# Attention with gated feed-forward on Trainium2: 41 maxima pieces a group in another order of pieces, and 68 instead of 55 ahead of the first score piece

## The reference

```python
xn = _layernorm(x, axis=-1)
s = _L0_attn_ref(xn, w_qkv, b_qkv, w_out, b_out)      # softmax(q k / 4 + alibi + causal) v, then w_out
g = _silu(_L0_ffn_ref(xn, w_gate, w_up, w_down))      # down(silu(gate(x)) * up(x)), ternary weights
x = x + s * g
```

## Time and profile before

| | us |
|---|---|
| median of 3 runs | 844.55 (843.7 to 845.68) |
| the profiled execution, its own time | 842.03 |
| its span in the trace | 840.0 |
| PE busy | 799.9 (95%) |
| DVE busy | 637.3 (76%) |
| ACT busy | 468.9 (56%) |

### The profile page before, as it was taken

The page is one execution under the profiler, slowest core; times in us unless marked ns, Lnnn a source line. Parts: engine busy times, 40 slices in busy tenths (PEclk is TensorE's granted clock), DMA queues, the critical chain, the costliest instruction groups (busy, mean ns, idle before and its releaser), DMA issues.

```text
span 840.0 us, 16103 instructions
## 1 busy us (share of the span) xinstructions
PE 799.9 (95%) x5926; PEld 352.8 (42%) x5926; DVE 637.3 (76%) x1822; ACT 468.9 (56%) x615; POOL 120.9 (14%) x136
## 2 busy tenths in 40 slices
PE   5999999999999999999899999999999999999998
PEld 3444545444444444444344343443434334343333
DVE  6656877733533565664899999999999999997546
ACT  5425275333132232222488888888888788787540
POOL 4213132223032131121000000000000005500000
PEclk9999999999999999999799999999999999999999
DMA  7474322358202101101121122222125333654636
GB/s 251 139 197 182 128 101 76 107 128 297 103 1 82 69 1 47 54 0 52 51 70 54 56 72 80 79 67 74 55 63 161 91 92 104 195 132 129 215 132 222
DMA packets 71055, 88.40 MB, mean 105 GB/s; under 512 B 26926, under 2 KB 37166, under 8 KB 70464
## 3 DMA queue, kind: packets, MB, share of 16 engines
q1 hardware_dynamic: 70848, 87.10, 32.4%
q0 software_dynamic: 128, 0.27, 0.2%
HBM read 51.15 MB, written 35.93 MB: 104 GB/s over the span
## 4 chain that ended last, share of the span: by engine, by line
PE 62%; DVE 23%; issue 7%; DMA 4%; ACT 3%; SPq 0%; POOL 0%; DVEq 0%; ACTq 0%
PE psum L1515 9%; PE psum L1492 9%; PE psum L1516 9%; DVE mx L1158 9%; DVE mshown L1154 8%; PE psum L1449 7%; PE psum L1526 5%; PE psum L1527 5%; PE psum L1467 2%; DVE mx L1154 2%; PE psum L1346 2%; PE psum L1348 2%; PE psum L1347 2%; PE psum L1550 1%; PE psum L1360 1%
## 5 line engine op out<-in xcount | busy, mean ns | idle before, releaser
L881 ACT ACTIVATE probs<-psum,exp_scale 128x1024 f32<-128x1024 f32 (+1 forms) x320 | 310.6, 1028 | 80.0 <-PE psum L1476 60.0
L1154 DVE CUSTOM_DVE_ANT_0 mshown<-psum,ahead 128x384 bf16<-128x384 f32 (+3 forms) x512 | 219.2, 487 | 1.4 <-PE psum L1449 0.4
L1449 PE MATMUL psum<-QKs 51*128 51x512 f16 (+3 forms) x768 | 189.0, 334 | 18.4 <-DVE mx L1158 6.2
L1492 PE MATMUL psum<-probs,Vs 128*32 128x512 f32 (+3 forms) x1536 | 162.1, 510 | 0.2 <-ACT probs L881 0.2
L1158 DVE TENSOR_REDUCE mx<-psum 128x1 f32<-128x512 f32 x256 | 157.6, 681 | 2.7 <-PE psum L1449 1.7
L1467 PE MATMUL psum<-QKs 53*128 53x512 f16 (+3 forms) x768 | 140.0, 331 | 1.6 <-ACT probs L881 1.4
L1515 PE MATMUL psum<-X,room 128*128 128x512 f16 (+1 forms) x352 | 133.6, 379 | 0.0
L1516 PE MATMUL psum<-X,room 128*128 128x512 f16 (+1 forms) x352 | 133.4, 379 | 0.0
L1449 PEld LDWEIGHTS psum<-QKs 51*128 51x128 f16 x768 | 51.9, 94 | 157.1 <-DVE mx L1154 85.6
L906 ACT ACTIVATE room<-psum,gate_half 128x512 f32<-128x512 f32 (+1 forms) x44 | 30.3, 688 | 101.2 <-PE psum L1516 101.2
L757 POOL TENSOR_TENSOR room<-room 128x512 f16<-128x512 f32 (+1 forms) x44 | 50.9, 1157 | 174.5 <-ACT room L911 174.5
(11 more groups left out here) (161 smaller groups left out, 912.7 us busy)
## 6 DMA issues: line engine op xcount, KB each, us to landing
o_scr<-osum SPq DMA_DIRECT2D x32, 256.0 KB, 3.1
QKs<-q_scr SPq DMA_DIRECT2D x96, 64.0 KB
QKs<-k_scr SPq DMA_DIRECT2D x96, 64.0 KB
q_scr<-qk_stage SPq DMA_DIRECT2D x16, 256.0 KB, 2.3
k_scr<-qk_stage SPq DMA_DIRECT2D x16, 256.0 KB, 2.2
v_scr<-v_stage SPq DMA_DIRECT2D x16, 256.0 KB, 2.1
Vs<-v_scr SPq DMA_DIRECT2D x16, 256.0 KB
probs<-in_L_attn_x SPq DMA_DIRECT2D x4, 1024.0 KB, 11.2
```

The costliest lines, as they stand in the source:

```text
L881: nc.scalar.activation(probs[n % PSLOTS][:, 2 * pair:2 * pair + 2, 0:COLS[n]], s_bank[pair][:, :, 0:COLS[n]], ACT.Exp, scale=exp_scale[:, ...
L1154: last = nc.vector.tensor_tensor_reduce(out=mshown[at % 2][:, cols], in0=m_bank[bank][:, cols], in1=ahead[:, CH - keys:], scale=1.0, scala ...
L1449: last = nc.tensor.matmul(tile[:, hh, :], Qs[s][rows, pair + hh, qb * P:(qb + 1) * P], Ks[s][rows, pair + hh, k0:k0 + keys], start=(hh == ...
L1492: last = nc.tensor.matmul(pv_bank[32 * h:32 * h + 32, CH - cols:CH], Vs[s][:, kb, h::QH], probs[n % PSLOTS][:, h, at:at + cols], start=(kb ...
```

## The change

`GROUP` has 41 M instead of 42, in another order with the 20 S and 10 P. The items no longer begin at the same place in each group: `line(t)` gives the first one, 25 items into quad 1 for group 0, 24 into quad 2 for group 1, and so on to 11 into quad 15 for group 14. So the items put between the tiles of the gated stage are 66 instead of 52, and with the M of group 0 that stand ahead of its first score piece 68 instead of 55. The number of items in the whole program, 672, and the instructions of each are unchanged.

```diff
-GROUP = "MPMMPSMMSMPMMSSMMMSSMMPMSMMSPMMSMPMM" \
-        "SMSMMPMSMMMMSSMPMMSPMMSSMMPMMSMSMMSM"
+GROUP = "MPMSMPMMPMSMMSMMSMMSMSMMMSMPMSMSMPM" \
+        "MPMSSMMPMSMMPMSMSMMPMMSSMMPMSMMSMSSM"
+AHEAD = [LEAD + (QUADS - 2 - t) * (NITEM - GROUP.count("M")) for t in range(QUADS - 1)]
+
+
+def line(t):
+
+    return (t + 1) * NITEM + AHEAD[t] if t < QUADS - 1 else QUADS * NITEM
...
-    items = [(t + 1, i) for i in range(LEAD, NITEM)] + [(t + 2, i) for i in range(LEAD)]
+    items = [divmod(i, NITEM) for i in range(line(t), line(t + 1))] if t < QUADS - 1 else []
+    if t == QUADS - 2:
+        items.append((QUADS, ROWS_AT))
...
-    early = [(0, i) for i in range(NITEM) if i != ROWS_AT] + [(1, i) for i in range(LEAD)]
+    early = [divmod(i, NITEM) for i in range(line(0)) if i != ROWS_AT]
```

More of the change, by code:

```diff
@@ L161, in group_order @@
             out.append(("products", *products.pop(0)))
-        else:
+        elif items:
             out.append(("maximum", *items.pop(0)))
-    return [w for w in out if w[1] >= 0 and (w[0] != "maximum" or w[1] < QUADS or w[1:] == (QUADS, ROWS_AT))]
+    return [w for w in out if w[1] >= 0]
 def work_order():
-    early = [(0, i) for i in range(NITEM) if i != ROWS_AT] + [(1, i) for i in range(LEAD)]
+    early = [divmod(i, NITEM) for i in range(line(0)) if i != ROWS_AT]
     tiles = [(j, p) for j in range(NCH) for p in range(FTILES)]
```

## The result

| | before | changed | ratio |
|---|---|---|---|
| median of the runs | 844.12 us (843.14 to 845.68) | 893.44 us (888.96 to 897.49) | 1.0579, 95% interval 1.055 to 1.0609 |
| span of the profiled execution | 840.0 | 890.9 | |
| mean granted clock of TensorE | 0.99 | 0.959 | |

The kernel is 49 us slower. Forecast were 20 us, 864.5 with a range up to 876. The direction was right, and both costs that were summed are there; the size was not, since what the sum left out, the clock above all, is larger than what it had.

A forecast was written before the change was run, and what follows sets the result against it. PE was taken to bound the gated stage and DVE the attention stage, with PE close behind. Terms 14.4 - 7.8 + 13.5 = +20.1 us on the median 844.55 gave 864.5, range 851 to 876.

The forecast's parts named there:

- both costs that were summed: Likeliest case: gated stage (14.4 us) and new order of pieces in attention (13.5) both cost; 856 to 869, chance 0.58.
- the clock: PE's clock might halve behind three new idle stretches in the gated stage, 4.5 to 15 us; left out of the sum.
- rival 3: The clock falls in the gated stage, or PE lags behind its banks in more places: 869 to 880, chance 0.15.
- 13 fewer items: Attention stage: 13 full tiles fewer behind the first score piece, 0.60 us each on the pace-setting engine: -7.8 us.
- (a): Gated stage: 11 more items ahead of the last tile, 0.18 us a fill and 0.1 a break: 2.2 us.
- (d): Behind the gated stage's last tile: six items instead of four, fifth and sixth waiting 0.61 us each: 1.2 us.
- (b): Gated stage: the fourth fill of portions behind three output tiles waits 3.23 us each, less 0.4: 9.3 us.
- (c): Gated stage: the fourth fill behind up tiles (2, 7) and (3, 7) waits 0.92 us each, less 0.13: 1.7 us.
- The covers: Attention: three banked items' reads must cover product piece and next fill; narrow items fall short, +13.5 us, bounds 4 to 18.
- The signs that the prediction named: Profile after: 3.2 us idle PE behind three output tiles, unequal attention groups; half clock between 320 and 400 for rival 3.
- The row item comes earlier than before in all groups but the last ones, with no cost: Attention stage: the row item's earlier place in the groups was priced at 0.
- What is hidden: Attention: ACT's work, the next quad's load and the row item stay covered; 0 taken for the load.

The follow-up runs named there:

- experiment 5: The changed kernel with 15 added matmuls on constants keeping PE busy ahead of each fill that waits about 3 us, at four places: 888.74 us, 1.0518.
- experiment 12: Changed kernel with gated-stage portions of three, fills in the stretch without products done twice, and the last rows' transpose eight pieces later: 862.29 us, 1.0218.
- experiment 1: The changed kernel with at most three items handed out between two tiles of the gated stage, all else as changed: 880.16 us, 1.0424.
- experiment 4: The kernel before with one portion of four behind output tile (2, 22), paid back by a portion of two behind tile (3, 0): 849.65 us, 1.0061.
- experiment 2: The changed kernel with portions of at most three in the gated stage and the old order of pieces less one maximum: 867.22 us, 1.0271.
- experiment 11: experiment 2 with the 41 tiles of maxima in another order, chosen to lower the count of late reads from 16.9 to 11.6 us: 864.61 us, 1.0248.
- experiment 3: The kernel before with the new order of pieces alone, 42 maxima a group, nothing sliding: 886.32 us, 1.0506.
- experiment 6: experiment 3 with the fills of the stretch without products done twice, 11 in each of groups 1 to 13: 862.18 us, 1.021.
- experiment 13: experiment 12 with the loads for GpSimd's first pass over the denominators issued three score-piece steps earlier: 864.31 us, 1.0241.

## Why the prediction was wrong

The step that failed is **the clock**. The prediction had seen that PE's clock fell to half behind the idle stretch at the end of the gated stage, and wrote of the three new ones: "It is a rival below", with nothing in the sum. For the attention stage it did not consider the clock at all. The runs put about 21 us there, as much as the whole forecast of 20; the other 10 us that were missed are spread over the table's five smaller differences.

| part of the 50.9 us | predicted | found |
|---|---|---|
| start, up to tile (2, 0) | 0 | 2.5 |
| gated stage without the clock | 14.4 | 15.6 (21.3 less the 5.7 of experiment 5) |
| half clock in the gated stage | rival 3 | 5.7 |
| half clock in attention | not foreseen | about 15 |
| wait for the last rows, group 14 | 0 | 2.1 |
| GpSimd's pass against DVE, group 12 | 0 | about 1.5 |
| attention, 13 fewer items and late reads | -7.8 + 13.5 = 5.7 | 8, the rest |

How the 15 come about: experiment 12 differs from experiment 1 in attention by -14.0 us (396.6 to 382.6). It has 2.1 us less of waiting for the rows, and its doubled fills cost 3.3 (groups 2, 4, 6 and 7, without half clock in either, are 0.21 to 0.24 longer, times 15). So 14.0 - 2.1 + 3.3 = 15.2 for 41 us less of half clock, 0.37 of each. Group 3 gives the same without a doubled fill: 25.93 with 3.4 us of half clock, 24.65 in experiment 5, where none fell into it, 0.38 of each. In the gated stage it is 5.7 of 13.6, 0.42; 1.1 of the 13.6 lie in a wait, where they cost nothing. In experiment 4, where all of it fell on PE's dense work, it was 1.7 of 3.4, one half. That attention has less than half fits with DVE setting the pace in part of it; this is argued, not measured. The terms are differences of single traces; I hold each to be good to about 1 us, an estimate.

**(a) and (d), more fills and two more items at the end:** right. 3.1 in experiment 1, where their prices give 3.2; the fifth and sixth item 0.60 each.

**(b) Portions of four behind output tiles:** right. Waits of 3.23, 2.97 and 3.23 us, 9.4 against 9.3; and one made alone in the kernel before gave 3.23. What was missing is what each sets off, some 2 us more.

**(c) Behind up tiles:** right. 0.78 and 0.96, 1.7 against 1.7.

**13 fewer items:** not measured by itself. DVE's busy time in a group fell by 0.4 us (24.02 to 23.6), where the step had 0.60, and its idle time in the five groups of the next paragraph rose from 0.23 to between 0.68 and 1.40: the item's time was given back and waits took it up again. No group is shorter than before.

**The covers:** right in kind, too low in size, and weak as a rule. In the five groups after group 0 that had no half clock the step gives 24.24 - 0.60 + 0.6, 0.8, 1.1, 0.5 and 0.7, that is 24.24, 24.44, 24.74, 24.14 and 24.34; measured were 25.00, 24.54, 25.08, 24.28 and 24.46, 0.3 more in the mean, the "further 0.3 in each group" of its upper bound. The waits of DVE for PE's fills in attention, as the traces have them, are 2.1 us before, 25.5 changed (with what the half clock adds), 16.2 in experiment 12 (no half clock after group 0, up to 3.3 from doubled fills) and 23.6 in experiment 2; the count had 1.2, 14.7, 14.7 and 16.9. With LEAD 14 it gave 1.7 for 1.97, with LEAD 22 0.6 for 1.60, and it did not rank two orders of items (experiment 11). It names the mechanism, but its error is as large as the differences between good alignments.

**The signs that the prediction named** were there: idle stretches of 3.2 ahead of fills, groups that differ, the shortest of them 6 and 7, half clock between 320 and 400. Groups 9 and 10 were to be about 25 us and took 26.74 and 28.13, with 3.4 and 6.8 us of half clock. The half clock was named as the mark of rival 3, and that is what came: rival 3 had 869 to 880 and a chance of 0.15, and its price, 5.7 us, is near the 4.5 that the prediction worked out for short falls. Alone it would have left the time within the range; the fall in attention took it out.

**"The row item comes earlier than before in all groups but the last ones, with no cost"** failed in its second half: no cover was named for the last group, where the row now stands directly behind the last item. And GpSimd was missing from "What is hidden" altogether: since the items slide, the closing instructions of a quad come at another time in each group, and one of them met GpSimd's pass.

**Why the clock falls in attention** is shown as far as the order goes: the new order alone does it in each group (experiment 3), the old one with sliding items does it hardly at all (experiment 2), and more matmuls in the stretch without products end it (experiment 6). The Trainium skill (TensorE: Matmul & The Clock Gate, "A second HAM failure mode: psum-queue depth-cycling") tells of a clock that swings because PE idles briefly between groups of matmuls. The trace is in keeping with it: from 510.1 to 517.3 PE was busy for 6.09 of 7.19 us, and no gap was longer than 0.4 us. In experiment 3, though, PE was busy for 6.22 of the 6.80 us ahead of the fall. What exactly brings the clock down there is not shown. The prediction drew on the section before that one, on long gaps, and looked for gaps of 3 us alone; for those the runs agree in the gated stage and do not at the start of attention (experiment 5).

## What to carry to other kernels

A gap of PE of some 3 us, or a thin stretch, can cost twice: what it lasts, and what the clock takes from the work behind it. Put both into the sum; here each microsecond of half clock cost about 0.4 us, and 0.5 where PE's work was dense. When an order of pieces is rewritten, look for the longest stretch in which PE is given little, and not only for waits. Where items slide against a fixed order, every place where they meet something else (a ring, a row, a load, another engine's pass) must be gone through for all groups, since each meets another one.

## What the hardware showed that I had not expected

- With nothing changed but the order of pieces, eight groups in a row took 27.28 to 27.31 us, each with 6.8 us at the clock's lower level in the same place: a fall of the clock can be part of a steady rhythm.
- Doing matmuls twice made a kernel 24 us faster (886.3 to 862.2), still slower than the kernel before.
- The half clock at the start of attention (10.2 us before) stayed when PE's idle stretch ahead of it was filled with matmuls (10.3, experiment 5).
- DVE's small instructions on SBUF took up to 1.20 us instead of 0.17 to 0.19 while GpSimd ran its tensor operations, which are 1.1 to 1.3 us each; DVE's reads of PSUM beside the same operations kept their 0.69. The Trainium skill has an exclusive lock on a port that the two engines share (SBUF — State Buffer, "SBUF: two separate sides"); experiment 13 agrees, since the delay moved with GpSimd's pass.
- With LEAD 14 and 22 the load of the last quad came 4.9 and 3.7 us late, once, though all groups before it had their loads in time.
